# A sparse mixture-of-experts layer on one core: seeded PSUM banks, another product order, and w1's sums on GpSimd

## The chip, the cores and the metric

One core of a Trainium2 chip runs the whole program. Its engines are TensorE (PE in the profile), VectorE (DVE), ScalarE (ACT), GpSimd (POOL) and SyncE (SP); they run side by side and wait for each other by semaphores. The metric is the device time of one execution in microseconds; for the kernel before, the median of three runs is 1593.59 us (1579.11 to 1599.36).

## The reference

4096 tokens of 512 float32 values pass a quaternion rotation (a fixed 4x4 mixing of the four 128-wide parts of a token, because the gate in the frequency domain is the same for every frequency), a router to 2 of 8 experts with a capacity of 1024 tokens each, and a two-layer network per expert:

```python
logits = xf @ gate_w.T                       # xf: the rotated tokens, 4096 x 512
topv, topi = jax.lax.top_k(softmax(logits), 2)
gates = topv / jnp.sum(topv, axis=-1, keepdims=True)
...                                          # loc: place within the expert; dropped from 1024 on
de = disp.reshape(E, cap, Dm)                # 8 x 1024 x 512
h = jax.nn.relu(jnp.einsum('ecd,ehd->ech', de, fc1_w) + fc1_b)   # H = 2048
eo = jnp.einsum('ech,ehd->ecd', h, fc2_w) + fc2_b
out = jnp.sum(gathered * (gates * w)[:, :, None], axis=1)
return x + out
```

## The kernel before, in words

The program has one function with a section of code for each engine; the order of the work on every engine is written out by hand. A start (routing, tables of token rows, the first expert's tokens) is followed by eight experts in turn. An expert's 1024 tokens are two slabs of 512.

Each float32 operand is split into a high part (rounded, made on ScalarE) and a low part (the rest, made on VectorE), and each product is hi·hi + hi·lo + lo·hi.

**First layer.** Eight groups g, each of two tiles of 128 hidden units, for both slabs. The 2x2 block product is done with seven products (Winograd's form) instead of eight: `product` at L960 is six matmuls. The operands on the weights' side are A22, A11, A12 and the sums S1 to S4, those on the tokens' side B11, B21, B22 and T1 to T4. Products p1, p6, p7, p4 accumulate in a running bank (0 or 3 by the group's parity), and are copied out at each stage (`s1`, `s2`, `s3`); p2 has bank 1, p5 and p3 share bank 2. VectorE adds: `c11` (L824) is p2 + bias + s1, `c22` (L834) is the half-finished bank 2 + bias + s3, `c12` (L853) the finished bank 2 + bias + s2. p3 waits for `c22`, p5 of the next group for `c12`. In its order of products a group is p2, p6, p5, p7, a step of the second layer, p1 of the next group, p4, p3, another step.

**Second layer.** `fc2(N)` (L970) is a step: 12 matmuls of one hidden tile against w2's high and low part. 32 steps an expert: 0 to 13 run between the products, the rest behind the groups. The results sum up in four banks (4 to 7 for the first slab, 0 to 3 for the second).

**Weights.** SyncE's queue loads w1 (8 DMAs a group, `load_cut`, L217) and w2 (one a step, three buffers; the load of N + 3 waits until step N's w2 is split, L252). VectorE turns w1 (`turn_w1`, L677), makes the sums S1 to S4 (`sum_w1`, L685, four instructions a group), ScalarE makes the high parts (`w1_high`, L426), VectorE the low ones (`w1_low`, L698).

**Tokens of the next expert (the reload).** They come in four units of 256 rows, numbered V = 4e + u, through the one buffer `x_blk`: GpSimd gathers the rows (`gather_x`, L346), SyncE stores them to a DRAM buffer (`store_x`, L258) and loads them back cut into 32-wide pieces (`cut_x`, L263, 8 DMAs), VectorE turns them (`turn_x`, L732), then ScalarE and VectorE rotate them into `yfull` (L457, L740) and split them in the second layer. `gather_x(V)` waits until unit V - 1 is turned. Units are turned in groups 1, 3, 5 and 7, in each case in front of `c22`.

**Output.** GpSimd gathers rows of the output and their gates (L355), VectorE adds the gated bias (`add_b2`, L767) and the gated result (`add_rows`, L774), GpSimd scatters them back (L365).

## Time and profile before

| | |
|---|---|
| median of 3 runs | 1593.59 us |
| the profiled execution's own time | 1585.56 us |
| its span, first to last instruction | 1583.8 us |
| TensorE busy | 1410.8 us (89%) |
| VectorE busy | 1180.5 us (75%) |
| ScalarE busy | 681.5 us (43%) |
| GpSimd busy | 373.3 us (24%) |
| mean granted TensorE clock | 0.961 of full speed |
| DMA | 200.46 MB, 455727 packets |

All times come from one execution recorded by the hardware profiler. Matmuls are pipelined: a matmul of 512 columns shows some 0.39 us, but the next one starts earlier, so starts are to be compared, not lengths. A line is a line of the kernel; a helper's line stands for all its calls. `SPq` is SyncE's DMA queue. "Idle before" is the time in which an engine did nothing just ahead of an instruction, with what ended it.

### The profile page before, as it was taken

What the parts mean: (1) busy time and instruction counts of PE and PEld (TensorE: products, weight loads), DVE (VectorE), ACT (ScalarE), POOL (GpSimd) and SP (SyncE); (2) the same over time, 40 slices, a digit from 0 to 9 for tenths busy, and PEclk for the clock granted to TensorE, in tenths of its full rate; (3) what the DMA queues carried; (4) which work ended last, traced back from release to release, by engine and by line L of the source; (5) the groups of instructions that cost most, each with busy time, mean ns of one, the idle gap of its engine ahead of it and who ended that gap; (6) DMA issues with size and microseconds to landing.
All of it is one profiled execution on the core that took longest, in us unless ns stands there. A gap on an engine that the chain in (4) does not pass through costs nothing.

```text
span 1583.8 us, 18277 instructions
## 1 busy us (share of the span) xinstructions
PE 1410.8 (89%) x6090; PEld 1130.0 (71%) x6090; DVE 1180.5 (75%) x1928; ACT 681.5 (43%) x1072; POOL 373.3 (24%) x294
## 2 busy tenths in 40 slices
PE   8537999899998998989988999999989999999997
PEld 5325777677776776767776777787768777778885
DVE  6786788687795778767786877887788777876653
ACT  5224444344452443533443444544445444544442
POOL 1050002540044200640016400242005400350022
PEclk9657999999999999999999999999999999999999
DMA  8453554565545644465454655456546555454232
GB/s 305 162 123 73 114 120 100 141 159 114 112 120 144 142 108 94 126 175 116 102 112 140 154 122 106 119 176 130 112 95 179 143 125 110 118 148 86 53 100 85
DMA packets 455727, 200.46 MB, mean 127 GB/s; under 512 B 398816, under 2 KB 401001, under 8 KB 453714
## 3 DMA queue, kind: packets, MB, share of 16 engines
q1 hardware_dynamic: 437538, 146.95, 40.0%
q0 software_dynamic: 18096, 52.35, 11.2%
q8 instruction: 49, 0.80, 0.2%
q14 instruction: 44, 0.36, 0.1%
HBM read 159.50 MB, written 39.98 MB: 126 GB/s over the span
## 4 chain that ended last, share of the span: by engine, by line
PE 30%; DVE 23%; issue 13%; SPq 13%; POOL 8%; DMA 8%; ACT 6%; another core or an unknown queue 0%; ACTq 0%; DVEq 0%; POOLq 0%
SPq L221 12%; DVE yfull L747 5%; PE ps L993 5%; PE ps L994 5%; PE ps L998 5%; DVE w1t L683 5%; DMA x_blk<-slots_dram 4%; PE ps L965 4%; PE ps L967 3%; PE ps L966 3%; POOL out L369 3%; POOL rows L358 3%; ACT yfull L455 2%; DVE w_lo L705 2%; POOL gate_now L361 1%
## 5 line engine op out<-in xcount | busy, mean ns | idle before, releaser
L965 PE MATMUL ps<-yc_hi,w1c_hi 128*128 128x512 f32 x896 | 357.5, 399 | 77.1 <-DVE h L853 20.7
L993 PE MATMUL ps<-w_hi,h_hi 128*128 128x512 f32 x960 | 381.7, 398 | 43.5 <-DVE w_lo L705 43.5
L994 PE MATMUL ps<-w_lo,h_hi 128*128 128x512 f32 x960 | 379.7, 396 | 0.0
L966 PE MATMUL ps<-yc_lo,w1c_hi 128*128 128x512 f32 x896 | 351.0, 392 | 0.0
L967 PE MATMUL ps<-yc_hi,w1c_lo 128*128 128x512 f32 x896 | 350.9, 392 | 0.0
L965 PEld LDWEIGHTS ps<-yc_hi,w1c_hi 128*128 128x128 f32 x896 | 169.4, 189 | 135.5 <-ACT s L497 28.4
L369 POOL DMA_INDIRECT out<-rows,scatter_row x64 | 131.2, 2051 | 568.7 <-DVE rows L778 555.9
L998 PE MATMUL ps<-w_hi,h_lo 128*128 128x512 f32 x960 | 259.8, 393 | 0.0
L436 ACT ACTIVATE w_hi<-w_raw 128x512 fp32r<-128x512 f32 x256 | 159.9, 625 | 215.6 <-PE ps L998 130.7
L993 PEld LDWEIGHTS ps<-w_hi,h_hi 128*128 128x128 f32 x960 | 183.4, 191 | 89.7 <-DVE w_lo L705 51.3
L705 DVE TENSOR_TENSOR w_lo<-w_raw,w_hi 128x512 fp32r<-128x512 f32 x256 | 175.7, 686 | 55.2 <-ACT w_hi L436 55.0
L430 ACT ACTIVATE w1c_hi<-w1t 128x1792 fp32r<-128x1792 f32 x64 | 109.0, 1703 | 242.6 <-DVE w1t L696 238.3
L994 PEld LDWEIGHTS ps<-w_lo,h_hi 128*128 128x128 f32 x960 | 183.7, 191 | 38.3
L998 PEld LDWEIGHTS ps<-w_hi,h_lo 128*128 128x128 f32 x960 | 183.0, 191 | 38.8
L967 PEld LDWEIGHTS ps<-yc_hi,w1c_lo 128*128 128x128 f32 x896 | 169.3, 189 | 36.1
L966 PEld LDWEIGHTS ps<-yc_lo,w1c_hi 128*128 128x128 f32 x896 | 169.5, 189 | 33.2
L351 POOL DMA_INDIRECT x_blk<-in_x,gather_row x56 | 54.6, 974 | 483.8 <-DVE x_turned L737 467.5
L747 DVE SCALAR_TENSOR_TENSOR yfull<-x_turned,rot,yfull 128x256 f32<-128x256 f32 x336 | 140.3, 480 | 35.3 <-ACT yfull L455 28.6
L700 DVE TENSOR_TENSOR w1c_lo<-w1t,w1c_hi 128x1792 fp32r<-128x1792 f32 x64 | 129.4, 2021 | 31.1 <-ACT w1c_hi L430 23.3
L358 POOL DMA_INDIRECT rows<-out,gather_row x64 | 93.8, 1466 | 40.6 <-DMA out<-rows,scatter_row 23.5
L764 DVE SCALAR_TENSOR_TENSOR h_lo<-h,h_hi 128x512 fp32r<-128x512 f32 x128 | 87.9, 687 | 15.6 <-ACT h_hi L543 13.6
L737 DVE STREAM_TRANSPOSE x_turned<-x_blk 128x512 f32<-128x512 f32 x56 | 36.5, 690 | 76.7 <-DMA x_blk<-slots_dram 76.7
(157 smaller groups left out, 1491.6 us busy)
## 6 DMA issues: line engine op xcount, KB each, us to landing
w_raw<-in_L_ffn_fc_w SPq DMA_DIRECT2D x256, 256.0 KB
w_raw<-in_L_ffn_fc_w SPq DMA_DIRECT2D x512, 64.0 KB
slots_dram<-x_blk SPq DMA_DIRECT2D x28, 512.0 KB, 3.8
x_blk<-slots_dram SPq DMA_DIRECT2D x224, 64.0 KB
out<-x_all SPq DMA_DIRECT2D x8, 1024.0 KB, 13.1
x_all<-in_x SPq DMA_DIRECT2D x7, 1024.0 KB, 13.6
b_bc<-in_L_ffn_fc_b POOLq DMA_DIRECT2D x8, 256.0 KB
x_all<-in_x SPq DMA_DIRECT2D x4, 256.0 KB, 4.7
```

The costliest lines, as they stand in the source:

```text
L221: eng.dma_start(part, cut[dq]).then_inc(arrived, 16)
L358: pool.indirect_dma_start(rows[:, b, :], None, out_rows, bass.IndirectOffsetOnAxis(ap=gather_row[:, at:at + 1], axis=0)).then_inc(rows_in, 16)
L369: pool.indirect_dma_start(out_rows, bass.IndirectOffsetOnAxis(ap=scatter_row[:, at:at + 1], axis=0), rows[:, b, :], None, bounds_check=TOK ...
L436: act.activation(w2_hi[:, N % 3, :], w2_raw[:, N % 3, :], ACT.Copy).then_inc(w2_hi_ready, 1)
L705: dve.tensor_tensor(w2_lo[:, N % 3, :], w2_raw[:, N % 3, :], w2_hi[:, N % 3, :].bitcast(F32), ALU.subtract).then_inc(w2_ready, 1)
L747: ins = dve.scalar_tensor_tensor(y, x_turned[:, :, j, :], rot[:, i, j:j + 1], y, ALU.mult, ALU.add)
L965: pe.matmul(bank, hi, yc_hi[:, y, q, :], start=first and q == 0, stop=False, skip_group_check=True)
L966: pe.matmul(bank, hi, yc_lo[:, y, q, :], start=False, stop=False, skip_group_check=True)
L967: ins = pe.matmul(bank, lo, yc_hi[:, y, q, :], start=False, stop=last and q == 1, skip_group_check=True)
L993: pe.matmul(eo_s[:, b, :], h_hi[:, c, blk], w2_hi[:, w, :], start=(tile == 0), stop=False)
L994: pe.matmul(eo_s[:, b, :], h_hi[:, c, blk], w2_lo[:, w, :], start=False, stop=False)
L998: ins = pe.matmul(eo_s[:, b, :], h_lo[:, c, blk], w2_hi[:, w, :], start=False, stop=False)
```

## The change

- **Seeds.** p1 + bias is written by ScalarE into bank 1 (`seed_c11`), and p2 accumulates onto it; the copy `s1` and VectorE's add `c11` go. Likewise ScalarE writes the bias b2 into the four result banks of a slab ahead of its first step (`seed_eo`), and VectorE's `add_b2` goes. Five extra matmuls once (`set_bits`) prepare those banks for accumulation. The copies b1_now go.
- **Product order.** A group is now p6, p2, a step, p7, p5, p1 of the next group, p4, p3, a step; an expert begins with p1 of its groups 0 and 1. The order of T1, T3, T4 and B22 in the buffers follows.
- **Rotations** are made for a slab (512 columns) at a time, not for a unit (256); `x_turned` holds two units.
- **Reload.** `store_x` is issued by GpSimd, not SyncE. The gathers, stores, cuts and turns move to other groups (below).
- **Output rows.** Gates are gathered for a whole expert at once; the two slabs' rows use separate buffers.
- **w1's sums** are made by GpSimd (`sum_w1`), not VectorE.

SyncE:

```diff
+            cut_x(0)
             for e in range(E):
                 for g in range(GROUPS):
-                    if e == 0 and g == 1:
-                        store_x(0)
+                    if not last and g == 2:
+                        cut_x(4 * e + 2)
+                    if e < E - 2 and g == 6:
+                        cut_x(4 * e + 4)
                     load_w2(N + 3)
-                    if e == 0 and g == 1:
-                        cut_x(0)
-                    if not last and g in (2, 4, 6):
-                        store_x(4 * e + g // 2)
                     load_w2(N + 4)
                     if G + 3 < E * GROUPS:
                         load_w1(G + 3)
-                    if not last and g in (2, 4, 6):
-                        cut_x(4 * e + g // 2)
+                    if not last and g == 0:
+                        cut_x(4 * e + 1)
+                    if not last and g == 4:
+                        cut_x(4 * e + 3)
...
-                    if e < E - 2 and k == 8:
-                        store_x(4 * (e + 1))
-                    if e < E - 2 and k == 11:
-                        cut_x(4 * (e + 1))
```

GpSimd:

```diff
+            def sum_w1(G):
+                pool.wait_ge(w1_T, 2 * (G + 1))
+                pool.tensor_tensor(w1t[:, 4, :], w1t[:, 0, :], w1t[:, 1, :], ALU.add).then_inc(w1_sums, 1)
+                pool.tensor_tensor(w1t[:, 6, :], w1t[:, 2, :], w1t[:, 0, :], ALU.subtract).then_inc(w1_sums, 1)
+                pool.wait_ge(w1_sums, 4 * G + 2)
+                pool.tensor_tensor(w1t[:, 5, :], w1t[:, 4, :], w1t[:, 2, :], ALU.subtract).then_inc(w1_sums, 1)
+                pool.wait_ge(w1_sums, 4 * G + 3)
+                pool.tensor_tensor(w1t[:, 7, :], w1t[:, 3, :], w1t[:, 5, :], ALU.subtract).then_inc(w1_sums, 1)
...
             for e in range(E):
-                if not last:
-                    for u in range(1, 4):
-                        gather_x(4 * e + u)
+                for g in range(GROUPS):
+                    G = e * GROUPS + g
+                    if not last and g < 2:
+                        gather_x(4 * e + g + 1)
+                    if G + 2 < E * GROUPS:
+                        sum_w1(G + 2)
+                    if not last and g < 2:
+                        store_x(4 * e + g + 1)
+                    if not last and g == 2:
+                        gather_gates(e + 1)
+                    if not last and g == 4:
+                        gather_x(4 * e + 3)
+                        store_x(4 * e + 3)
+                    if e < E - 2 and g == 5:
+                        gather_x(4 * e + 4)
+                        store_x(4 * e + 4)
                 scatter_rows(2 * e)
+                if not last:
+                    load_b2(e + 1)
+                pool.wait_ge(h_ready, e * STEPS + HT + ROWS1 + SB)
                 gather_rows(2 * e + 1)
                 scatter_rows(2 * e + 1)
                 if not last:
                     gather_rows(2 * e + 2)
```

ScalarE:

```diff
+            def seed_c11(G):
+                e, g = G // GROUPS, G % GROUPS
+                act.wait_ge(p1_done, G + 1)
...
+                act.activation(ps[:, BANK_C11, :], running(G), ACT.Identity, bias=b1T[:, e * HT + 2 * g:e * HT + 2 * g + 1]
+                               ).then_inc(c11_seeded, 1)
+            def seed_eo(s, b):
+                act.wait_ge(b2_in, 16 * (s // 2 + 1))
+                act.activation(ps[:, EO[s % 2] + b, :], b2_bc[:, :], ACT.Copy).then_inc(eo_seeded, 1)
...
                     if G + 2 < E * GROUPS:
                         w1_high(G + 2)
+                    if not last and g == 1:
+                        first_of_slab(e + 1, 0)
+                    if not last and g == 5:
+                        first_of_slab(e + 1, 1)
```

VectorE, a group:

```diff
                     dve.wait_ge(p2_done, G + 1)
-                    dve.wait_ge(s1_ready, G + 1)
-                    dve.scalar_tensor_tensor(s1[:, :], ps[:, BANK_P2, :], b1_now[:, 2 * g:2 * g + 1], s1[:, :],
-                                             ALU.add, ALU.add).then_inc(c11_done, 1)
-                    if G >= 1 and G + 1 < E * GROUPS:
-                        w1_low(G + 1)
-                    low_of(N, s1[:, :])
+                    low_of(N, ps[:, BANK_C11, :])
                     w2_low(N)
-                    if not last and g % 2 == 1:
-                        turn_x(4 * e + g // 2)
+                    if not last:
+                        if g < 2:
+                            turn_x(4 * e + g)
+                        elif g < 5:
+                            rotate(e + 1, 0, g - 1)
+                        elif g == 5:
+                            turn_x(4 * e + 3)
+                        else:
+                            rotate(e + 1, 1, g - 5)
                     dve.wait_ge(p5_done, G + 1)
                     dve.wait_ge(s3_ready, G + 1)
...                  # c22
                     w2_low(N + 1)
+                    if not last and g == 4:
+                        turn_x(4 * e + 2)
                     if G + 2 < E * GROUPS:
                         turn_w1(G + 2)
-                        sum_w1(G + 2, 0)
+                    dve.wait_ge(p3_done, G + 1)
...                  # c12, then h_lo of tile N + 1
                     if G + 2 < E * GROUPS:
-                        sum_w1(G + 2, 1)
+                        w1_low(G + 2)
```

TensorE, an expert:

```diff
             for e in range(E):
-                p1(e, 0)
+                p1(e * GROUPS)
+                p1(e * GROUPS + 1)
                 for g in range(GROUPS):
-                    product(A12, B21, par, ps[:, BANK_P2, :], True, True, p2_done)
+                    pe.wait_ge(c11_seeded, G + 1)
                     product(S2, T2, par, bank, False, False, p6_done)
+                    if G:
+                        p2(G)
+                    if g:
+                        fc2(N - 2)
+                    product(S3, T3, par, bank, False, False, p7_done)
                     product(S1, T1, par, ps[:, BANK_P5, :], True, False, p5_done)
-                    product(S3, T3, par, bank, False, False, p7_done)
-                    if g:
-                        fc2(N - 2)
-                    if g < GROUPS - 1:
-                        p1(e, g + 1)
+                    if 1 <= g < GROUPS - 1:
+                        p1(G + 1)
                     product(A22, T4, par, bank, False, True, p4_done)
                     product(S4, B22, par, ps[:, BANK_P5, :], False, True, p3_done)
                     if g:
                         fc2(N - 1)
```

## Rows read from the trace of the kernel before

**Rows 1.** The page, part 1: busy time (share of the span), instructions.

```profile
PE 1410.8 (89%) x6090; PEld 1130.0 (71%) x6090; DVE 1180.5 (75%) x1928; ACT 681.5 (43%) x1072; POOL 373.3 (24%) x294
```

**Rows 2.** Windows, expert 0, 1, 3, 4, 6, 7: start:end, length, then the head's columns.

```profile
core 0: us, PE busy (x) PEld busy (x) DVE busy (x) ACT busy (x) POOL busy (x), PEclk, DMA share, GB/s
102.73:317.14 214.41, 175.43 (x721) 140.07 (x721) 159.60 (x259) 85.86 (x133) 41.51 (x27) 0.91 0.46 106
317.14:502.46 185.32, 168.89 (x722) 135.82 (x720) 140.98 (x228) 81.06 (x128) 50.88 (x34) 0.98 0.54 127
...
690.02:877.20 187.18, 169.19 (x722) 135.79 (x721) 140.89 (x228) 81.17 (x128) 50.48 (x34) 0.98 0.52 124
877.20:1055.20 178.00, 167.80 (x722) 135.51 (x721) 141.13 (x228) 81.27 (x128) 40.80 (x34) 0.99 0.56 135
...
1232.38:1408.70 176.32, 166.68 (x721) 134.19 (x720) 140.91 (x228) 81.39 (x128) 44.12 (x32) 1.00 0.53 123
1408.70:1572.47 163.77, 163.50 (x721) 134.87 (x719) 98.82 (x148) 66.46 (x102) 28.27 (x26) 1.00 0.36 90
```

**Rows 3.** Groups of instructions: busy, mean ns, idle just before them and its releasers.

```profile
L993 PE MATMUL ps<-w_hi,h_hi 128*128 128x512 f32 x960 | 381.7, 398 | 43.5 <-DVE w_lo L705 43.5
...
L965 PE MATMUL ps<-yc_hi,w1c_hi 128*128 128x512 f32 x896 | 357.5, 399 | 77.1 <-DVE h L853 20.7 <-ACT s L497 18.6 <-ACT s L468 17.1
```

**Rows 4.** TensorE's timeline, a window behind it, and a wait of SyncE's queue.

```profile
864.78 0.79 PE L993 MATMUL ps<-w_hi,h_hi 128*128 128x512 f32 x1 [5.96 <-DVE w_lo L705]
...
863.30:870.20 6.90, 5.42 (x12) 3.79 (x12) 3.83 (x6) 0.00 (x0) 0.35 (x1) 0.51 0.64 218
...
SPq L260 <- DMA x_blk<-in_x,gather_row: 88.0, 6, 18.4
```

**Rows 5.** Timelines of SyncE, VectorE and TensorE, expert 0, group 1: start, length.

```profile
139.18 0.56 SPq L261 DMA_DIRECT2D slots_dram<-x_blk  x1
...
142.57 5.33 SPq L221 DMA_DIRECT2D x_blk<-slots_dram  x8
...
150.42 1.31 DVE L737 STREAM_TRANSPOSE x_turned<-x_blk 128x512 f32<-128x512 f32 x2 [8.27 <-DMA x_blk<-slots_dram]
151.65 0.71 DVE L834 SCALAR_TENSOR_TENSOR h<-ps,b_now,s 128x512 f32<-128x512 f32 x1
...
152.41 0.79 PE L965 MATMUL ps<-yc_hi,w1c_hi 128*128 128x512 f32 x1 [5.90 <-DVE h L834]
```

**Rows 6.** The reload: GpSimd's, SyncE's and VectorE's timelines; landings of L351, L261, L343.

```profile
152.00 0.95 POOL L351 DMA_INDIRECT x_blk<-in_x,gather_row  x1 [42.23 <-DVE x_turned L737]
153.25 0.95 POOL L351 DMA_INDIRECT x_blk<-in_x,gather_row  x1 [0.30 <-issue]
...
698.59 0.58 POOL L392 DMA_DIRECT2D b_bc<-in_L_ffn_fc_b  x1 [2.04 <-DMA out<-rows,scatter_row]
...
801.22 5.39 SPq L221 DMA_DIRECT2D x_blk<-slots_dram  x8
...
808.46 1.30 DVE L737 STREAM_TRANSPOSE x_turned<-x_blk 128x512 f32<-128x512 f32 x2 [4.03 <-DMA x_blk<-slots_dram]
...
DMA to landing us min/median/max: 3.2/3.5/4.6
...
DMA to landing us min/median/max: 3.1/3.8/4.0
...
DMA to landing us min/median/max: 3.2/3.2/3.2
```

**Rows 7.** Groups of instructions again, then the scatter's line: ns min/median/max.

```profile
L430 ACT ACTIVATE w1c_hi<-w1t 128x1792 fp32r<-128x1792 f32 x64 | 109.0, 1703 | 242.6 <-DVE w1t L696 238.3 <-issue 4.3
...
L497 ACT ACTIVATE s<-ps 128x512 f32<-128x512 f32 x64 | 37.7, 589 | 66.5 <-PE ps L967 66.5
...
L331 POOL MEMSET carry<- 128x512 f32 x1 | 0.5, 525 | 0.1
...
L330 POOL MEMSET ones<- 128x128 f32 x1 | 0.2, 218 | 0.0
...
L369 POOL DMA_INDIRECT out<-rows,scatter_row x64: 982/1023/10043, 267.2 to 1576.1; - x64
```

More of the change, by code:

```diff
@@ L77, in program @@
         gate_row = sb("gate_row", [P, BLOCKS], I32)
+        gates = sb("gates", [P, BLOCKS])
         gm = sb("gm", [P, TJ, E])
@@ L256, in load_w2 @@
                 sp.dma_start(w2_raw[:, N % 3, :], w2_rows[row:row + P, :]).then_inc(w2_in[N % 3], 16)
-            def store_x(V):
-                for bb in range(2):
-                    sp.wait_ge(blk_in[bb], 16 * (V + 1))
-                sp.dma_start(slots_dram[V % 2].rearrange("b p d -> p b d"), x_blk[:, :, :]).then_inc(cut_out, 16)
             def cut_x(V):
```

358 lines of the change are left out of this document (188 added, 170 removed).

## The prediction

> **What bounds the kernel now.** I read the busy shares first: TensorE is busy 89% of the span [rows 1]. Then the span cut at the first matmul of each expert [rows 2]. The last expert runs its 720 matmuls in 163.8 us, 0.2275 us each, with almost nothing in the way, so a product of the first layer (6 matmuls) is 1.36 us and a step of the second (12) is 2.73. Over 163.8 us the experts cost, in order, 50.6, 21.5, 23.8, 23.4, 14.2, 13.4 and 12.5 us (the third and sixth from the edges of their neighbours' rows): 159.5 us in all. That is all that an order of work can win in the main part, and the change adds or removes almost no matmul. So the question is which waits go and which come.
>
> The groups of matmuls with what ended the idle time before them name the waits [rows 3]. The largest, 43.5 us, is for w2's low part. Its source is SyncE's queue: `store_x` at k = 8 waits for a gather that GpSimd has not yet issued (88.0 us in six waits [rows 4]), w2's loads stand behind it, and TensorE idles 5.96 us at the 30th step. Behind that idle the granted clock is 0.51 and twelve matmuls take 5.4 us in place of 2.7 [rows 4]: a long idle costs some 2.6 us more than itself. The 20.7 us (`c12`, L853) and 18.6 us (s2's copy, L497) are VectorE coming late to P5's evacuation in groups 2, 4, 6. The 17.1 us come once, at the start.
>
> **What the change takes away.** (a) `store_x` leaves SyncE and every `cut_x` leaves the second layer, so w2's prefetch is not held: 5.96 idle and 2.6 clock, 8.6 us, in each of the first four experts, which is about what they cost more than the next three (23.4 against 14.2 [rows 2]). (b) P5's evacuation gets p2, an fc2 step and p7, 5.4 us, before S1·T1 wants the bank: the waits on L853 and L497 go, some 6 to 8 us an expert. (c) Each group's four w1 sums, one add of L824, and `add_b2` leave VectorE; this hides behind matmuls and I cost it at nothing. (d) Start: ScalarE makes the seed before the late high copies, but TensorE still needs T2's low copy, ScalarE now has four `eo` seeds in between, and five matmuls set bits. Of the 29.1 us that expert 0 costs over expert 1, 8.2 are a wait in its group 1 (5.90 [rows 5] and 2.3 of clock), the rest, some 20.5, is the start. Between 0 and 17.1 can go; I take 2, near the lower end, because the rotations before T2 are unchanged.
>
> **What it adds: a reload that has one group.** x_blk is a single buffer: turn, gather, store, cut, and the next turn are serial. Before, units were turned in groups 1, 3, 5, 7; now in 0, 1, late 4 and 5, and in 1 and 5 the turn stands in VectorE's queue ahead of `c22`, for which S4·B22 (p3) waits. Expert 0 shows this already [rows 5]: store at 139.18, first cut at 142.57, turned at 150.42, `c22` at 151.65, TensorE released at 152.41 after 5.90 us. From first cut to turn is 7.9 us (8 issues of one queue and a landing), from turn to TensorE 2.0.
>
> The links of the chain [rows 6]: two gathers 1.25 us apart, landing 3.5 us after the second: 4.75. Store: 3.8 us to landing from SyncE for these same bytes; from GpSimd 3.2 for a quarter of them (128 KB). I take 3.8, the same transfer, and 0.3 for the issue. Cut to turn 7.9. Turn end (151.72) to first gather (152.00) 0.3 [rows 5, 6]. Sum 17.1 us.
>
> *Group 0 to 1.* Count from the expert's first matmul. Group 0 is 8 products, 10.9 us; in group 1 p3 is due after six products and one step, at 21.8. GpSimd has the last scatter's landing behind it only at 8.6 (698.59 against 690.02) [rows 2, 6]; 0.3 and four row gathers at the 1.25 of a gather bring it to 13.9. So the gathers for unit 4e+1 issue at 14.0 and 15.2, landing 18.7. In between GpSimd makes group 2's sums, 16.5 to 19.5 (below); store landed 23.6, turned from 31.5, TensorE released 33.5: 11.7 us late. s2's copy, queued on ScalarE behind w1's high copy (sums 19.5, copy 1.7, s2 0.6 [rows 7]), is late too, but within these 11.7.
>
> *Group 4 to 5.* VectorE turns unit 4e+2 behind `c22` and w2's copy, ending about 10.9 into the group, then turns w1, 12.2. GpSimd's program puts the sums first: 15.2; gathers 15.5 and 16.8, landing 20.3; store 24.4; turn 32.3; release 34.2. p3 of group 5 is due at 15.0 + 10.9 = 25.9: 8.4 us late.
>
> What queues behind the late turn: `c22`, w2's low part, w1's turn, so GpSimd's sums, ScalarE's w1 copy and `first_of_slab` (four 128x512 copies), behind which the next group's s2 stands: 0.9 us for both places together. Each of the two idles is longer than the 5.96 us that lost the clock, so 2.6 us each. At the start of the second layer VectorE still has a rotation (now full width) and four `add_rows` beside the low parts of the steps; some steps wait for those today, too. I keep 2 us for it, between nothing and 5 for eight more instructions of some 0.7 us with no slack.
>
> **The price of a w1 sum on GpSimd** is not in the trace. Nearest rows: a memset of 128x128 takes 218 ns and of 128x512 525 [rows 7], so 0.12 us and 0.8 ns a column. A sum of 256 columns touches three tensors: 0.32 us if all overlap, 0.73 if not. I take 0.73, since it reads two tensors, and with semaphore waits 3.0 us for four; they could cost as little as 1.3. In an ordinary group VectorE is idle until p3 is done (12.2 to 12.4). Turned w1 at 12.2, sums 15.2, high copy 17.0, low copy 19.0, while the next c12, p7 and `low_of` want ScalarE and VectorE only around 19 to 20.4: hidden. If that cover were gone, each us would cost a us in nearly every group.
> The Trainium skill, "GPSIMD Engine Reference", section 3.1, measures a float32 add of 2048 columns at 4497 ns on GpSimd, about twice VectorE; scaled to 256 columns an estimate of 0.56 us each, by which the four are 2.3 us, the two late releases come up to 0.7 us earlier each, and the total would be some 9 us lower. No row here shows it.
>
> **The sum.** Experts 1 to 6: 11.7 + 8.4 + 2 x 2.6 + 0.9 + 2.0 = 28.2 each, 169. Expert 0: start 18.5, group 1 unchanged at 8.2 (GpSimd is free there, the turn comes at nearly the same time), group 5 11.6, second layer 2: 40.3. Expert 7 reloads nothing, but its sums for group 2 come at 16.7, so s2 is 3 us late: 3. In all 212 us in place of 159.5: +53. The profiled execution took 1585.56 us (span 1583.8 and 1.8 around it); its time becomes 1639. The median of the three runs is 8 us higher (1593.59). I say **1640**.
> Bounds: with all links at their shortest [rows 6] (gather 3.2, store 3.1, cut 801.22 to turn 808.46 = 7.2, sums 1.3, clock 1 each) the two late releases are 8.9 and 5.5 and an expert costs 20: about 1585. With links at their longest (gather 4.6, store as long, cut 8.6, as far above the 7.9 as 7.2 lies below, sums 4, 3.4 of clock each) 36: about 1690.
>
> **Rivals.**
> *A, faster: the reload fits.* Place: the turn in groups 1 and 5. With the two late releases gone, 18.5 + 8.2 + 7 x 2 + 4 = 45 us stay and the time is 1470; with them halved, 1560. It decides where the chain is under 13 us: then the removed waits win. For it: GpSimd no longer gathers gates between rows, SyncE waits less. Against: even the shortest instances of the links sum to 15, and expert 0 shows the same wait ending where TensorE's does. 0.18.
> *B, GpSimd becomes the bound.* w1 turned at 12.2, s2 of the next group wanted at 20.4, less 0.7 and 1.8: the four sums have 5.5 us, 1.4 each. At 1.9 each, every group of the first layer is 2 us late, 56 x 2: 1750. For it: a scatter issue takes 1.0 us in the middle and 10.0 at most [rows 7], so GpSimd can be held up. Against: twice the dearest bound from the memsets, and VectorE is idle just then. 0.09.
> The Trainium skill, "SBUF — State Buffer", section "Who interferes with whom", says that GpSimd and VectorE share one port pair as an exclusive lock, which a VectorE instruction with two SBUF inputs takes for its whole length. By it the low copies and rotations would block the sums and be blocked by them. That speaks against this move; no row before shows GpSimd arithmetic.
> *C, gain and loss cancel*: the short ends, 1585 to 1610. 0.10.
> Forecast: 0.63.
>
> **Numbers.** From no change 2% can be told: 1562 to 1626 against the median. The forecast's own range is 1610 to 1690, most of it above 1626. Range for 8 in 10: 1560 to 1700; outside lie A without its halved case and most of B. Slower: 0.8 of the forecast, B: 0.59. Same: the rest of the forecast and C: 0.23. Faster: 0.18.
>
> **What would show it.** Right: TensorE's top wait is for `c22` in groups 1 and 5 of seven experts, two per expert of 7 to 12 us, with VectorE's turn waiting for x_blk<-slots_dram; no wait for w2's low part late in the second layer; the last expert near 167 us. GpSimd adds at 0.5 to 0.8 us. Wrong: the turn's wait under 5 us (then A), or TensorE waiting for s2 in every group (then B).

## The result

The kernel after takes **1628.88 us** (median of 4 runs, 1627.52 to 1631.48), the kernel before on the same chip 1592.28: a ratio of 1.0301, 95% interval 1.0251 to 1.0350. It is slower by 3%. (The ratios leave out executions in which the chip was in a slower state, the medians don't; by the medians it is 2.3%.) I had said 1640, with 1560 to 1700 as the range. The profiled execution took 1628.14 us, its span is 1626.4; before it was 1583.8, so 42.6 us came in.

The page of the kernel after, part 1, and its stretches by expert (the columns are those of [rows 2]; experts 0, 1, 3, 6, 7):

```profile
PE 1431.7 (88%) x6095; PEld 1152.5 (71%) x6095; DVE 995.7 (61%) x1384; ACT 705.6 (43%) x1072; POOL 586.7 (36%) x570
```

```profile
101.70:306.50 204.80, 178.14 (x724) 143.34 (x725) 137.74 (x188) 90.84 (x136) 79.08 (x73) 0.90 0.48 113
306.50:496.50 190.00, 171.02 (x722) 138.51 (x721) 117.37 (x157) 84.10 (x127) 74.51 (x69) 0.95 0.52 124
...
687.10:878.70 191.60, 171.51 (x722) 138.87 (x721) 117.29 (x157) 84.02 (x127) 74.75 (x69) 0.95 0.51 123
...
1260.60:1449.80 189.20, 169.75 (x722) 137.65 (x721) 117.39 (x157) 84.11 (x127) 70.42 (x66) 0.95 0.48 115
1449.80:1614.50 164.70, 163.53 (x722) 135.08 (x721) 77.54 (x108) 68.59 (x106) 38.10 (x40) 1.00 0.34 88
```

Set beside [rows 1, 2]: VectorE has 185 us less work, and yet each of experts 1 to 6 now takes about 190 us (before: 176 to 188). Only expert 0 became shorter (214.4 to 204.8). Experts 1 to 3 became 3 to 5 us longer, experts 4 to 6 13 us each. The last one, which reloads nothing, is 0.9 us longer.

Where TensorE's idle time went, by the groups of instructions (columns as in [rows 3]; L1021 is a product's first matmul, L1044 a step's):

```profile
L1021 PE MATMUL ps<-yc_hi,w1c_hi 128*128 128x512 f32 x896 | 365.2, 408 | 120.6 <-DVE h L899 100.8
L1044 PE MATMUL ps<-w_hi,h_hi 128*128 128x512 f32 x960 | 385.4, 401 | 13.0 <-DVE w_lo L767 10.6
```

Against [rows 3] the wait for w2's low part fell from 43.5 to 10.6 us, and the one for `c12` (20.7) is gone. In their place stands `c22` (L899): 100.8 us. The waits of the kernel after say how often (engine, line, what ended the wait: us in total, times, longest):

```profile
DVE x_turned L802 <- DMA x_blk<-slots_dram: 140.0, 14, 12.0
...
PE ps L1021 <- DVE h L899: 100.8, 14, 8.6
PE ps L1021 <- ACT s L548: 19.8, 8, 3.4
```

Fourteen times is twice in each of seven experts. The wait for s2's copy was 18.6 us before, in groups 2, 4 and 6; now it stands in group 1. The first of the two for `c22`, group 1 of expert 3, in order of time (timeline of the kernel after: start, length, engine, instruction, [idle before]):

```profile
699.28 0.95 POOL L360 DMA_INDIRECT x_blk<-in_x,gather_row  x1 [0.30 <-issue]
700.54 0.95 POOL L360 DMA_INDIRECT x_blk<-in_x,gather_row  x1 [0.30 <-issue]
701.51 0.74 POOL L348 TENSOR_TENSOR w1t<-w1t 128x256 f32<-128x256 f32 x1
...
703.83 0.73 POOL L353 TENSOR_TENSOR w1t<-w1t 128x256 f32<-128x256 f32 x1
704.59 1.70 ACT L468 ACTIVATE w1c_hi<-w1t 128x1792 fp32r<-128x1792 f32 x1 [6.11 <-POOL w1t L353]
706.20 0.58 ACT L548 ACTIVATE s<-ps 128x512 f32<-128x512 f32 x1
...
706.83 0.50 PE L1021 MATMUL ps<-yc_hi,w1c_hi 128*128 128x512 f32 x1 [2.63 <-ACT s L548]
707.18 0.77 POOL L367 DMA_DIRECT2D slots_dram<-x_blk  x1 [2.62 <-DMA x_blk<-in_x,gather_row]
711.50 5.54 SPq L228 DMA_DIRECT2D x_blk<-slots_dram  x8
...
719.51 1.30 DVE L802 STREAM_TRANSPOSE x_turned<-x_blk 128x512 f32<-128x512 f32 x2 [9.96 <-DMA x_blk<-slots_dram]
720.74 0.71 DVE L899 SCALAR_TENSOR_TENSOR h<-ps,b1T,s 128x512 f32<-128x512 f32 x1
721.09 0.99 POOL L360 DMA_INDIRECT x_blk<-in_x,gather_row  x1 [13.14 <-DVE x_turned L802]
...
721.50 0.79 PE L1021 MATMUL ps<-yc_hi,w1c_hi 128*128 128x512 f32 x1 [7.29 <-DVE h L899]
```

Read it from the end: TensorE waits for `c22`, `c22` stands behind the turn on VectorE, the turn waits for the cut, the cut for the store, the store for the gathers. The 2.63 us at 706.83 are a second wait of the same group: s2's copy stands on ScalarE behind w1's high copy, which waits for GpSimd's last sum.

### The profile page after: what moved, and what is told of

It is laid out like the page before. It is cut to its first block, busy times and chain, and to the rows that moved or that the text cites. A ratio compares the mean times of both kernels' runs of the same rounds, so it can differ in the third digit from the quotient of the medians.

```text
span 1626.4 us, 17933 instructions
## 1 busy us (share of the span) xinstructions
PE 1431.7 (88%) x6095; PEld 1152.5 (71%) x6095; DVE 995.7 (61%) x1384; ACT 705.6 (43%) x1072; POOL 586.7 (36%) x570
## 4 chain that ended last, share of the span: by engine, by line
PE 59%; DVE 14%; DMA 10%; POOL 7%; issue 4%; SPq 4%; ACT 1%; DVEq 0%; POOLq 0%; ACTq 0%
PE ps L1044 11%; PE ps L1045 11%; PE ps L1049 10%; PE ps L1021 8%; PE ps L1023 8%; PE ps L1022 8%; DMA x_blk<-in_x,gather_row 4%; SPq L228 4%; DMA slots_dram<-x_blk 3%; DMA x_blk<-slots_dram 2%; POOL rows L380 2%; DVE w_lo L767 2%; DVE h L838 1%; DVE yfull L823 1%; DVE w1t L745 1%
## 5 line engine op out<-in xcount | busy, mean ns | idle before, releaser
L1021 PE MATMUL ps<-yc_hi,w1c_hi 128*128 128x512 f32 x896 | 365.2, 408 | 120.6 <-DVE h L899 100.8
L1044 PE MATMUL ps<-w_hi,h_hi 128*128 128x512 f32 x960 | 385.4, 401 | 13.0 <-DVE w_lo L767 10.6
L1022 PE MATMUL ps<-yc_lo,w1c_hi 128*128 128x512 f32 x896 | 361.3, 403 | 0.0
L1023 PE MATMUL ps<-yc_hi,w1c_lo 128*128 128x512 f32 x896 | 360.8, 403 | 0.0
L1021 PEld LDWEIGHTS ps<-yc_hi,w1c_hi 128*128 128x128 f32 x896 | 175.2, 196 | 168.7 <-DVE h L899 106.7
L762 DVE TENSOR_TENSOR w1c_lo<-w1t,w1c_hi 128x1792 fp32r<-128x1792 f32 x64 | 129.6, 2025 | 186.5 <-ACT w1c_hi L468 176.2
L1044 PEld LDWEIGHTS ps<-w_hi,h_hi 128*128 128x128 f32 x960 | 186.2, 194 | 64.2 <-DVE w_lo L767 19.5
L348 POOL TENSOR_TENSOR w1t<-w1t 128x256 f32<-128x256 f32 x62 | 46.1, 743 | 441.4 <-DVE w1t L745 440.2
L1023 PEld LDWEIGHTS ps<-yc_hi,w1c_lo 128*128 128x128 f32 x896 | 175.7, 196 | 38.2
L1022 PEld LDWEIGHTS ps<-yc_lo,w1c_hi 128*128 128x128 f32 x896 | 175.8, 196 | 36.0
L388 POOL DMA_INDIRECT out<-rows,scatter_row x32 | 83.1, 2597 | 135.7 <-DVE rows L838 128.4
L811 DVE SCALAR_TENSOR_TENSOR yfull<-x_turned,rot,yfull 128x512 f32<-128x512 f32 x168 | 114.8, 747 | 0.0
L511 ACT ACTIVATE ps<-ps,b1T 128x512 f32<-128x512 f32 x64 | 42.3, 661 | 145.7 <-PE ps L1023 134.5
```

Source lines behind the costliest of these rows:

```text
L762: dve.tensor_tensor(w1c_lo[:, G % 2, :, :], w1t[:, 1:8, :], w1c_hi[:, G % 2, :, :].bitcast(F32), ALU.subtract).then_inc(w1_ready, 1)
L811: ins = dve.scalar_tensor_tensor(y, x_turned[:, :, j, :], rot[:, i, j:j + 1], y, ALU.mult, ALU.add)
L1021: pe.matmul(bank, hi, yc_hi[:, y, q, :], start=first and q == 0, stop=False, skip_group_check=True)
L1022: pe.matmul(bank, hi, yc_lo[:, y, q, :], start=False, stop=False, skip_group_check=True)
L1023: ins = pe.matmul(bank, lo, yc_hi[:, y, q, :], start=False, stop=last and q == 1, skip_group_check=True)
L1044: pe.matmul(eo_s[:, b, :], h_hi[:, c, blk], w2_hi[:, w, :], start=False, stop=False, skip_group_check=True)
```

## The experiments

Each was measured beside the kernel before, whose medians were 1579.22 us (for the first four experiments), 1575.55 (the next four), 1569.82 (row gathers behind the store, two kernels) and 1589.0 (the last two). So the kernel before itself moves by up to 20 us from set to set. Where two changed kernels of different sets are compared by their times, differences of 20 us and less rest on the traces, not on the times. A number given for a "wait" of TensorE is, in expert 3 unless said, how much longer than its bare 1.36 us the product that waited took (2.73 for a step), counted from the start of the last matmul ahead of it to the start of its own last: the idle time and what its own matmuls lost on the lower clock. So 7.29 us idle is a wait of 8.6. p7 and p3 are the products that wait for s2's copy and for `c22`.

**One part alone: the store by GpSimd.** The kernel before, and of the change only this for the first unit of an expert:

```diff
-                    if e < E - 2 and k == 8:
-                        store_x(4 * (e + 1))          # SyncE
...
                     gather_x(4 * (e + 1))
+                    store_x(4 * (e + 1))              # GpSimd
```

> The kernel before, with one edit: the store of each next expert's first unit is issued by GpSimd right behind its gathers, not by SyncE at k = 8; its cut stays on SyncE at k = 11, behind the load for the next expert's step 0. If SyncE's wait for that gather is what starves w2 (my reading), TensorE's waits at the 30th and 31st step of experts 0 to 3 and 6 go: 4 x 10.3 + 1.6 = 43 us less, about 1549 against 1592. If GpSimd's late gathers matter by another way (SyncE now waits at the cut in place of the store), the wait only moves to the next expert's first steps and the time stays within 10 us of before.

Measured 1565.35 us, ratio 0.9916 (0.9875 to 0.9957): 13.9 us below the kernel before, a third of the 43 that I expected, and less than 2%. Experts 1, 2 and 3 became 7.5, 10.3 and 9.1 us shorter (177.8, 177.3, 178.1), and their late wait in the second layer is gone. In expert 0 it stayed (5.89 us idle), and expert 6 became 7.7 us longer (184.0) by a late wait of 5.83 us that it did not have before. The VectorE timeline of expert 0 says why:

```profile
301.85 0.75 DVE L779 SCALAR_TENSOR_TENSOR rows<-b_bc,gate_now,rows 128x512 f32<-128x512 f32 x1 [8.79 <-DMA gate_now<-gates_dram,gate_row]
...
303.12 0.69 DVE L713 TENSOR_TENSOR w_lo<-w_raw,w_hi 128x512 fp32r<-128x512 f32 x1
```

and GpSimd's of the same run, what held the gates up:

```profile
283.49 7.52 POOL L360 DMA_INDIRECT rows<-out,gather_row  x1 [2.98 <-DMA out<-rows,scatter_row]
```

`add_b2` waits 8.79 us for gates that GpSimd gathers behind a row gather whose issue took 7.5 us; w2's low part stands behind it. Expert 6 shows the same wait of 8.7 us.

The kernel before has this wait in all of its first four experts. Expert 3, GpSimd's timeline and then VectorE's, just ahead of the 5.96 us at 864.78 [rows 4]:

```profile
828.35 10.04 POOL L369 DMA_INDIRECT out<-rows,scatter_row  x1 [0.30 <-issue]
...
844.70 7.17 POOL L358 DMA_INDIRECT rows<-out,gather_row  x1 [3.33 <-DMA out<-rows,scatter_row]
```

```profile
862.77 0.75 DVE L771 SCALAR_TENSOR_TENSOR rows<-b_bc,gate_now,rows 128x512 f32<-128x512 f32 x1 [8.84 <-DMA gate_now<-gates_dram,gate_row]
863.44 0.68 DVE L764 SCALAR_TENSOR_TENSOR h_lo<-h,h_hi 128x512 fp32r<-128x512 f32 x1
864.04 0.68 DVE L705 TENSOR_TENSOR w_lo<-w_raw,w_hi 128x512 fp32r<-128x512 f32 x1
...
870.87 0.69 DVE L705 TENSOR_TENSOR w_lo<-w_raw,w_hi 128x512 fp32r<-128x512 f32 x1 [3.75 <-ACT w_hi L436]
```

So the 5.96 us end with `add_b2`, not with a load of w2. The load that the store held comes only after it: ScalarE's copy waits for it, VectorE's low part at 870.87 for that, TensorE another 1.35 us. In both kernels the wait of 5.8 to 6.0 us stands in exactly those experts in which a scatter's issue took 10.0 us and the row gather's behind it 7.2 to 7.7: 0 to 3 before, 0 and 6 here. In the others the scatter's took 3.6 us (10.0 once in each kernel) and that row gather's 1.0 to 1.1, and an expert takes 176 to 178 us whether SyncE or GpSimd issues the store (experts 4 and 5: 178.0 and 177.2 before, 177.0 and 176.2 here). The store itself is thus worth about 1 us there. Whether its move is also why experts 1 to 3 lost their long issues and expert 6 got them, this run doesn't show. The change removes both waits: `add_b2` is gone, and no store stands in SyncE's queue.

**Undo one part: group 5.** The kernel after, with unit 4e+3 turned in group 6 instead of 5, the next expert's first gather and store in group 6, its cut in group 7, and the rotations behind them one place later:

```diff
-                        elif g == 5:
+                        elif g == 6:
                             turn_x(4 * e + 3)
```

> The changed kernel, with unit 4e+3 turned one group later (group 6 in place of 5), its first term with it, the first rotation of that slab in group 7 and the second in group 7 too, ahead of w1's low part. If the chain of one buffer inside one group is the cause: the waits of p3 in group 5 (9.2 to 9.9 us, with 0.4 to 1.8 us behind them, seven experts) go, 7 x 11 = 77 us less, about 1552 against the changed kernel's 1629; the waits of group 1 stay. If the loss came from w1's sums on GpSimd or from the seeds, nothing that matters is touched and the time stays within 10 us of 1629.

Measured 1560.54 us, ratio 0.9875 (0.9792 to 0.9959). The wait in group 5 is gone in all seven experts, which are 8.6 to 10.5 us shorter; the first step of the second layer now waits 1.5 us, a rotation standing ahead of it.

**Undo both.** The same, and unit 4e+1 turned in group 2 instead of 1:

```diff
-                        if g < 2:
-                            turn_x(4 * e + g)
+                        if g in (0, 2):
+                            turn_x(4 * e + g // 2)
```

> As the last, and unit 4e+1 is turned in group 2 in place of 1 (first term behind it, rotations in groups 3, 3 and 4). Its sums on GpSimd, the seeds, the product order and the wide rotations are those of the changed kernel. If the two one-group chains are all that makes it slower: both waits go, 7 x (11 + 13) = 168 us less, less some small new waits: 1465 to 1485, which is faster than the kernel before by 7 to 8%. If GpSimd's sums are a second bound, s2 stays late in the groups and the time stays above 1530.

Measured 1494.63 us, ratio **0.9458** (0.9378 to 0.9538). One group of room at two places turns 3% slower into 5% faster. Expert 2 there, against 190.6 in the kernel after:

```profile
460.50:630.90 170.40, 164.93 (x722) 134.64 (x721) 118.01 (x156) 83.90 (x127) 76.26 (x70) 1.00 0.57 138
```

The time was some 10 us above my range: 2.9 us before p7 in group 1 stayed in each expert that reloads.

**Undo one part: the sums back on VectorE.** The kernel after, all four behind the turn of w1:

```diff
-                    if G + 2 < E * GROUPS:
-                        sum_w1(G + 2)                 # GpSimd
...
                         turn_w1(G + 2)
+                        for n in range(3):
+                            sum_w1(G + 2, n)          # VectorE
```

> The changed kernel with w1's sums back on VectorE, directly behind the turning of w1; the reload is as changed. My theory: the sums on GpSimd cost only where they stand inside the reload's chain: in group 0 to 1 the second gather's store comes 2.2 us earlier, in group 4 to 5 the gathers start 3.0 to 4.5 us earlier, so the two waits shrink to about 5 each: 30 to 45 us less, 1585 to 1600. If the shared port or GpSimd's pace were the main loss, nearly all of the 160 us of waits would go: under 1510. If the sums don't matter at all: 1629.

Measured 1591.53 us, ratio 1.0074 (1.0032 to 1.0115). The wait in group 5 fell from 9.6 to 6.6, the 3.0 us of four sums. In group 1 the two waits became one:

```profile
707.19 0.79 PE L1021 MATMUL ps<-yc_hi,w1c_hi 128*128 128x512 f32 x1 [9.95 <-DVE h L897]
```

In experts 1 to 6 the store of group 0 was still issued 6.3 to 7.75 us after the second gather (6.4 to 7.7 in the kernel after), with no sum beside it: the sums are not what makes that landing long.

**Another order on GpSimd.** The kernel after, the store ahead of the sums:

```diff
                         gather_x(4 * e + g + 1)
-                    sum_w1(G + 2)
                         store_x(4 * e + g + 1)
+                    sum_w1(G + 2)
```

> The kernel after, with GpSimd's order in groups 0 and 1 of an expert turned round: gather, store, then the four w1 sums (in the kernel after the sums stand between the gathers and the store). Nothing is left out. In group 1 the store was issued 7.3 us after the turn that freed x_blk, in group 2 5.2 to 5.7. Theory 1 (the store waits for its gathers' data, which land late there for another reason, so the sums in between are hidden): the store moves by less than 0.5 us, and the sums now start behind it, some 6 us later than before; the high copy of w1 then comes 4 to 6 us later in groups 0 and 1, p7 of the next group waits 4 to 6 us more: 1635 to 1665 us. Theory 2 (the sums delay the store by their own 3.0 to 3.4 us): the wait for c22 in group 1 shortens by 2 to 3 us an expert and the time falls to 1600 to 1615.

Measured 1663.41 us, ratio 1.0583 (1.0500 to 1.0666): slower than the kernel after, as theory 1 has it. The store waits for landing data and the sums behind it come late, so s2 is late in two groups:

```profile
731.90 0.80 PE L1021 MATMUL ps<-yc_hi,w1c_hi 128*128 128x512 f32 x1 [9.07 <-ACT s L548]
753.85 0.54 PE L1021 MATMUL ps<-yc_hi,w1c_hi 128*128 128x512 f32 x1 [4.25 <-ACT s L548]
```

**Both units later and the sums on VectorE.** The edits of the third and the fourth experiment together.

> The kernel with units 4e+1 and 4e+3 turned one group later, and w1's four sums back on VectorE behind the turn of w1 (as in the kernel before, but all four in one place). Nothing is left out. Theory 1 (with the reload off the path, the move of the sums to GpSimd is worth nothing or less than nothing, because VectorE has the idle time for them and GpSimd adds them at the end of a chain at the start of each expert): the 2.9 us wait ahead of p7 in group 1 of seven experts goes, and the time falls from 1494.6 to 1465 to 1485 us. Rival (VectorE was the limit, and the sums hold up h_lo or c12): new waits of 1 us or more in most groups, 1510 to 1560.

Measured **1474.25 us**, ratio **0.9383** (0.9309 to 0.9457), the fastest of all. Expert 3:

```profile
622.90:789.60 166.70, 164.65 (x722) 134.76 (x721) 126.98 (x188) 84.22 (x127) 49.18 (x38) 1.00 0.60 141
```

This expert is 2.9 us longer than the bare 163.8, all of it in the first steps of the second layer; experts 1 to 3 and 5 take 166.7 to 167.3. Experts 4 and 6 take 171.7 and 168.2, with 3.1 and 1.2 us idle before p7 in group 3. VectorE has 9 us more to do in an expert than with the sums on GpSimd, and TensorE waits less.

**Double the suspected cost.** The third experiment's kernel, with four more sums on GpSimd in each group:

```diff
+                for t in range(2):
+                    link(pool.tensor_tensor(w1t[:, 4, :], w1t[:, 0, :], w1t[:, 1, :], ALU.add))
+                    link(pool.tensor_tensor(w1t[:, 6, :], w1t[:, 2, :], w1t[:, 0, :], ALU.subtract))
```

> The kernel with units 4e+1 and 4e+3 turned one group later, with four extra sums of the same shape on GpSimd in front of the high copy in every group (each repeated add and subtract writes what it had written; the result is the reference's). It costs what is claimed to be hidden: the four sums take some 3.0 to 3.4 us, and four more add as much. Theory 1 (my rival B's threshold: from turned w1 to the s2 copy of the next group the four sums have 5.5 us): 6.4 to 6.8 us in all are 1 to 1.5 us too many in the 7 or 8 groups of each expert, 56 x 1.2 = 67 more with some lower clock: 1545 to 1585 us. If ScalarE's order has more slack than that (8 us or more), the time stays within 1495 to 1510; if the sums were on the path already, every added us counts, 64 x 3.2 = 205: 1680 to 1720.

Measured 1651.24 us, ratio 1.0509 (1.0425 to 1.0592): 157 us for 3.3 us more in a group, where I expected 50 to 90. (With the four extra ones beside them, GpSimd's sums take 0.7 to 1.2 us each.) TensorE waits for s2 in group 1 (7.2 us) and in 3, 4, 5 and 7 (1.4 to 2.8):

```profile
719.85 0.80 PE L1030 MATMUL ps<-yc_hi,w1c_hi 128*128 128x512 f32 x1 [5.83 <-ACT s L551]
...
754.79 0.50 PE L1030 MATMUL ps<-yc_hi,w1c_hi 128*128 128x512 f32 x1 [1.87 <-ACT s L551]
```

and 7.7 us at the first step of the second layer, where w1's high copy stands on ScalarE ahead of the seeds and that step's w2. The room for four sums is real but smaller than my 5.5 us, above all where GpSimd has gathers in front of them or ScalarE has other work behind.

**The order on ScalarE.** The third experiment's kernel, w1's high copy for group 2 behind s2's copy of group 1:

```diff
                     act.activation(s2[:, :], running(G), ACT.Copy).then_inc(s2_ready, 1)
+                    if g == 1:
+                        w1_high(G + 1)
...
-                    if G + 2 < E * GROUPS:
+                    if g and G + 2 < E * GROUPS:
                         w1_high(G + 2)
```

> The kernel with units 4e+1 and 4e+3 turned one group later, and on ScalarE the high copy of w1 for group 2 of each expert is made behind the copy s2 of group 1, not ahead of it. Nothing is left out. Theory 1 (p7 in group 1 waits only because s2 is queued behind that high copy, which waits for GpSimd's last sum): the 2.9 us wait goes in seven experts, down to under 0.8, and the time falls from 1494.6 to 1472 to 1482 us. Rival (the high copy is itself late, and p1 of group 2, 3 us behind p7, waits for it in place of p7): the wait moves to p1 or p4 of group 1 with 1 to 3 us, 1488 to 1496.

Measured 1486.22 us, ratio 0.9451 (0.9376 to 0.9526). The rival was nearer: p7's wait is gone and the next p1 waits 1.8 us for w1's low copy instead (1.50 us idle):

```profile
653.35 0.50 PE L1029 MATMUL ps<-yc_hi,w1c_hi 128*128 128x512 f32 x1 [1.50 <-DVE w1c_lo L764]
```

So all of what follows the sums is late here, not s2 alone. (In expert 1 there is a wait of 4.2 us in group 3 besides, whose cause I did not follow.)

**What GpSimd issues ahead.** The kernel after, its four row gathers for the next expert moved behind the store of group 0; the same in the third experiment's kernel; and once more in the kernel after, but into group 3:

```diff
+                    if e and g == 0:                  # third kernel: g == 3
+                        gather_rows(2 * e)
...
-                if not last:
-                    gather_rows(2 * e + 2)
```

> The kernel after, with GpSimd's four gathers of output rows for the next expert's first slab moved from the end of an expert to group 0 of the next one, behind the sums and the store there. Nothing is left out. In the kernel after these four gathers (4 x 1.27 us to issue) stand between the scatter and the gathers for x_blk: the latter start 2.9 us after the turn that frees x_blk (508.66 against 505.73 at expert 2), and land 6.7 to 7.4 us after the second in place of 4.4. Theory 1 (both come from the row gathers ahead of them): the chain of unit 4e+1 becomes 4 to 5 us shorter, the wait for c22 in group 1 falls from 8.6 to 3 to 5 us, and the one ahead of p7 from 2.9 to under 1 (the sums follow the gathers): 6 to 7.5 us for each of six experts, 1628 down to 1580 to 1592. Rival (the slow landing has another cause, the traffic of w1 and w2 at that time): the issue alone is 2.7 us earlier, some 4 us an expert with the one ahead of p7, 1600 to 1608.

> The kernel with units 4e+1 and 4e+3 turned one group later (sums on GpSimd), with the same move of the row gathers. Nothing is left out. There the first sum of group 0 starts at 644.88 in expert 3 though w1 was turned at 642.1, since GpSimd is still issuing gathers. Theory 1 (the 2.9 us wait ahead of p7 in group 1 comes from what GpSimd issues ahead of the sums, not from the 0.74 us of a sum): the wait falls to under 0.8 in experts 1 to 6, 1494.6 down to 1472 to 1482, level with the version with the sums on VectorE (1474.3). Rival (the sums themselves, 3.0 us and the handing on from engine to engine, are too long for this place): the wait stays at 1.5 to 3, 1486 to 1496.

> The kernel after, with the four gathers of output rows moved to group 3 of the next expert, where GpSimd has nothing else but its sums (in the run before they stood behind the store in group 0). Nothing is left out. In that run the data of the gathers for x_blk landed 4.3 to 5.1 us after the second one instead of 6.4 to 7.4, but the cut that follows took 9.7 us from its first DMA to the turn instead of 7.4, and only 1.6 to 2.4 us an expert were left of the gain. Theory 1 (1 MB of row gathers delays whichever transfer of the reload it runs beside, by 2.2 to 2.7 us): beside neither, landing stays at 4.3 to 5.1 and the cut goes back to 7.2 to 7.6; the wait for c22 in group 1 falls from 8.9 to 6.2 to 6.9, and the time from 1616.1 to 1597 to 1606 us. Rival (the cut is slow because it now starts earlier and meets w1's loads): the cut stays at 9.2 us or more, 1611 to 1620.

Measured 1616.13 us (ratio 1.0296, 1.0244 to 1.0347), 1481.74 (0.9430, 0.9383 to 0.9477) and 1611.30 (1.0165, 1.0109 to 1.0220). The first misses both theories. Expert 3 in it:

```profile
693.85 0.97 POOL L360 DMA_INDIRECT x_blk<-in_x,gather_row  x1 [0.30 <-issue]
...
698.93 0.77 POOL L367 DMA_DIRECT2D slots_dram<-x_blk  x1 [0.53 <-DMA x_blk<-in_x,gather_row]
700.01 1.00 POOL L380 DMA_INDIRECT rows<-out,gather_row  x1 [0.30 <-issue]
...
702.36 6.84 SPq L228 DMA_DIRECT2D x_blk<-slots_dram  x8
...
712.01 1.30 DVE L802 STREAM_TRANSPOSE x_turned<-x_blk 128x512 f32<-128x512 f32 x2 [8.62 <-DMA x_blk<-slots_dram]
```

and in the one with the row gathers in group 3:

```profile
695.79 0.97 POOL L360 DMA_INDIRECT x_blk<-in_x,gather_row  x1 [0.30 <-issue]
701.19 0.77 POOL L367 DMA_DIRECT2D slots_dram<-x_blk  x1 [0.82 <-DMA x_blk<-in_x,gather_row]
704.69 5.55 SPq L228 DMA_DIRECT2D x_blk<-slots_dram  x8
712.28 1.31 DVE L802 STREAM_TRANSPOSE x_turned<-x_blk 128x512 f32<-128x512 f32 x2 [6.91 <-DMA x_blk<-slots_dram]
```

From the second gather to the store: 6.64 us in the kernel after, 5.08 and 5.40 here. From first cut to turn: 8.01 in the kernel after, 9.65 with the row gathers beside the cut, 7.59 with them elsewhere. Over experts 1 to 6 the means are 6.9, 5.1 and 5.3 us for the first link, 7.6, 9.7 and 7.8 for the second. The megabyte of row gathers delays whichever transfer of the reload it runs beside, by some 1.5 to 2 us: the kind of thing that theory 1 of the third run says, though less than its 2.2 to 2.7. The time of that run lies in the rival's range all the same. The wait for `c22` in group 1 did fall, from 8.9 to 7.3 us on average, but the one in group 5 rose from 9.3 to 9.8 and expert 0 became 1.9 us longer; why is not shown. In the kernel with the later units the move takes p7's wait from 2.9 to 1.65 us. Its time is at the upper edge of theory 1's range, its wait in the rival's, so what GpSimd issues ahead is a part of that wait and not all of it:

```profile
646.90 0.50 PE L1027 MATMUL ps<-yc_hi,w1c_hi 128*128 128x512 f32 x1 [1.36 <-ACT s L548]
```

**Sums first.** The third experiment's kernel, with the sums ahead of the gathers for x_blk and the row gathers in group 1:

```diff
+                    sum_w1(G + 2)
                     if not last and g in (0, 2):
                         gather_x(4 * e + g // 2 + 1)
-                    sum_w1(G + 2)
-                    if not last and g in (0, 2):
                         store_x(4 * e + g // 2 + 1)
+                    if e and g == 1:
+                        gather_rows(2 * e)
```

> The kernel with units 4e+1 and 4e+3 turned one group later, with the sums on GpSimd put ahead of the gathers for x_blk in groups 0 and 2, and the four gathers of output rows moved to group 1 of the next expert, behind its sums. Nothing is left out. Theory 1 (a w1 sum on GpSimd costs nothing as long as GpSimd issues nothing ahead of it once w1 is turned): the 1.65 us wait ahead of p7 in group 1 that was left with the row gathers moved goes as well, 1481.7 down to 1466 to 1475 us, level with the sums on VectorE (1474.3). The later store (by 3.3 us) has 5 us of room before the turn in group 2. Rival (the handing on over GpSimd costs time by itself there): 0.8 us or more stay ahead of p7, or a new wait of 1 us or more comes in group 2: 1478 to 1486 us.

Measured 1509.63 us, ratio 0.9518 (0.9465 to 0.9571): a miss for both. Before p7 of group 1 only 0.8 us are left, but p7 of group 3 waits 2.7 to 5.7 us in all seven experts. Timelines, expert 3, of SyncE's queue and VectorE:

```profile
666.77 5.54 SPq L228 DMA_DIRECT2D x_blk<-slots_dram  x8
672.36 2.33 SPq L263 DMA_DIRECT2D w_raw<-in_L_ffn_fc_w  x2
674.74 7.06 SPq L228 DMA_DIRECT2D w_raw<-in_L_ffn_fc_w  x8
```

```profile
684.77 0.71 DVE L744 STREAM_TRANSPOSE w1t<-w_raw 128x512 f32<-128x512 f32 x1 [2.66 <-DMA w_raw<-in_L_ffn_fc_w]
```

The cut waits for the later store on SyncE's queue, w1's load stands behind the cut, VectorE's turn of w1 waits for it, and the sums come late, p7 of group 3 with them. Expert 0 shows this by itself, for its row gathers are not in group 1: its cut starts 4.3 us later than in the third experiment's kernel (42.9 us behind its first matmul against 38.6), and p7 of group 3 waits 2.7. In experts 1 to 6 the cut and the load start only 0.5 to 3.4 us later, but the load's eight DMAs take 6.2 to 8.7 us to issue where they took 4.7. That is the stretch into which this edit put the row gathers as well. The run moved two things at once, and what each cost in these experts is not separated. I had counted the room before the turn, and neither what is queued behind the cut nor what the row gathers would now run beside.

## Why the prediction was right

**Step (a), the second layer.** Right in that the wait goes and in its size, wrong in its cause. I had read 5.96 us idle and 2.6 of clock as SyncE's store holding w2's loads. The trace of the kernel before has `add_b2` there, waiting 8.8 to 8.9 us for gates that GpSimd gathered late, in the same four experts; the store is behind the 1.2 to 1.7 us that follow. It came out because the change removes both. That is luck: an edit of the store alone, which my reading priced at 43 us, gave 14. It also touches step (c), where I costed `add_b2` at nothing.

**Step (b), P5's evacuation.** No wait of half a microsecond is left in groups 2, 4 and 6. Its size was not measured by itself. What can be measured is all that the change takes away: with the reload and the sums out of the way expert 3 costs 2.9 us over 163.8 in place of 23.4, a gain of 20.5 in that expert. From the prediction's own terms it is 23.4 less the 0.9 and 2.0 that were to stay: 20.5.

**The reload chain.** The links of group 1, counted from the expert's first matmul (687.50 in expert 3), predicted and measured:

| | predicted | measured |
|---|---|---|
| gathers issued | 14.0, 15.2 | 11.8, 13.0 |
| sums | 16.5 to 19.5 | 14.0 to 17.1 |
| store issued | 19.5 | 19.7 |
| first cut | 23.6 | 24.0 |
| turn | 31.5 | 32.0 |
| TensorE released | 33.5 | 34.0 |
| late, with the clock's part | 14.3 | 14.0 |

The end was met because two errors cancel, which is luck for the links between. The gathers start 2.2 us earlier, since GpSimd has the last scatter behind it at 6.7 us and not at 8.6, but the store can go only 6.6 us after the second one, where I had 3.5 for the landing and the sums as the later of the two: GpSimd's row gathers run ahead of them. I had counted these four gathers' issue, not their bytes. The 14.0 are the gaps of p7 (2.9), p3 (8.6) and the products and the step that run on the lower clock behind them (2.4). In group 5 I had 8.4 + 2.6 = 11.0; measured 9.6 + 1.5 = 11.1. The clock behind the long wait, and in the same number of microseconds without one (windows of the kernel after, PEclk is the third from last):

```profile
721.40:728.20 6.80, 6.70 (x21) 5.39 (x22) 3.52 (x6) 2.13 (x2) 5.01 (x7) 0.70 0.72 164
751.00:757.80 6.80, 6.80 (x32) 5.63 (x31) 3.81 (x6) 2.78 (x4) 5.12 (x6) 1.00 0.48 88
```

At 0.2275 us each 6.8 us hold 30 matmuls; the first window has 21 (p3's six, the step's twelve and three of the next product, so none is missing), 2.0 us less.

**The cause of the loss is shown**, not only its timing: taking the one late turn away gave 68 us back, the other 66 more.

**The w1 sums.** Priced 0.73 us; measured 0.735, 0.736, 0.741 and 1.062 in the middle (the four in order), 3.05 to 3.6 us for all, 3.4 in the middle. The estimate by the Trainium skill, "GPSIMD Engine Reference", section 3.1, 0.56 us, was low here: this trace has 0.735. "Hidden in an ordinary group" holds in the kernel after. At the start of an expert and inside the reload's chain they are not: sums on VectorE take 3.0 us from the wait in group 5 of the kernel after, and are worth 20 us in the kernel whose reload fits (1494.6 to 1474.3). Much of that can be had with the sums still on GpSimd: the profiled spans are 1490.0 us, 1480.9 with the row gathers moved behind them, and 1471.6. Expert 7's part was 0.9 us, not 3.

**Second layer.** 3.1 us for the four waits in place of 2. **Start.** In the fastest kernel expert 0 is 186.1 us, 19.4 above an expert in the middle; I had 18.5.

**The sum.** The experts cost 202 us over 163.8 each, predicted 212: expert 0 41.0 (40.3), experts 1 to 6 26.8 on average (28.2), expert 7 0.9 (3). That is 10 of the 11 us between 1640 and 1629. (The short bound of the second release, 5.5 in the prediction, comes to 4.9 with its own links, which moves the lower bound by a few us.)

**The rivals.** A wanted a chain under 13 us; from the end of one turn to the start of the next it took 19 to 23. But its time for a reload that fits, 1470, is what the kernel with two later turns and VectorE's sums gives (1474). B did not decide: a sum was 0.74 and not above 1.4 (its own terms, 20.4 - 12.2 - 0.7 - 1.8, give 5.7 us for the four, not 5.5). The doubled sums show that it would have, earlier and harder than my arithmetic. C fell with the interval.

## What to carry to other kernels

Before work is moved off a busy engine, ask what the order of a single-buffered chain leaves for it: this change could take 20.5 us out of expert 3 and gave 25 back in two places where a turn stood one group too early in front of an addition that TensorE needed. Lay out such a chain link by link from one instance in the trace and compare it with the time at which its end is due; the end of the chain was good to half a microsecond here, with help from two errors that cancelled. When a link is moved, look at the queue that it waits in, not only at its own room: in expert 0 of the last experiment a cut that started 4.3 us later cost 2.7 us two groups on, through a load that had nothing to do with it. And where a wait ends with an instruction, look at what stands ahead of that instruction on its engine, before its operand's transfer is blamed: w2's low part was late behind `add_b2`, and I had blamed the queue that loads w2.

## What the runs showed of the hardware

**VectorE and GpSimd get in each other's way, by a third of a microsecond.** The kernel after, timeline of both (L912 reads two tensors in SBUF):

```profile
699.46 0.68 DVE L912 TENSOR_TENSOR h_lo<-s,h_hi 128x512 fp32r<-128x512 f32 x1
...
725.13 0.99 DVE L912 TENSOR_TENSOR h_lo<-s,h_hi 128x512 fp32r<-128x512 f32 x1
725.66 1.07 POOL L353 TENSOR_TENSOR w1t<-w1t 128x256 f32<-128x256 f32 x1
```

Alone VectorE's subtraction takes 0.68 us and GpSimd's 0.73 (at 703.83 above); overlapping, 0.99 and 1.07. The one that contends is the subtraction with two inputs in SBUF; `c12` at 724.47, which reads PSUM, left the sums beside it at 0.73, and over the whole trace the 38 sums that met `c12` alone took 0.72 to 0.74, the 55 that met the subtraction alone 1.06 to 1.07. The Trainium skill, "SBUF — State Buffer", section "Who interferes with whom", says that a VectorE instruction with two SBUF inputs contends with a GpSimd instruction that reads SBUF: the trace agrees. In the prediction I had put it as a lock for the whole length of an instruction. The rows don't bear that out; they show 0.3 us on each side, and the first was lengthened as well as the second, which started inside it.

**A megabyte of indirect gathers is felt by its neighbours.** Ahead of the two gathers for x_blk it put the store off from 4.6 to 5.7 us behind the second one (experts 1 to 6, row gathers behind the store) to 6.4 to 7.7 (kernel after); beside a cut it made 9.2 to 10.4 us of 7.4 to 8.2. The reason for the spread within these is not shown.

**An indirect DMA's issue can hold GpSimd for 7 to 10 us** (the scatter at 828.35 and the row gathers at 844.70 and 283.49 above) where most take 0.95. It is not spread at random: in the kernel after it is one scatter (7.2 to 7.7 us) and the first row gather behind the scatters (5.1 to 6.7) in each of seven experts, 14 of 256 issues; in the kernel before five experts have the long scatter and four of them the long gather too. Nothing in these runs shows why.
